# A Perceiver block on one core: contexts applied in one run, norm factors by ScalarE's root, and the copy of keys inside the maximum

## What is computed

```python
# cross attention: sublayers 1, 7 and 10 (a_cross, e_cross, t_cross), 16 heads of 8
att = softmax(einsum('bxhd,byhd->bhxy', q, k) * scale)    # 257 keys for each sequence
x = einsum('bhxy,byhd->bxhd', att, v) @ Wout + bout

# linear transformer: sublayer 2 (l), six layers deep, 8 heads of 16
q = softmax(q, axis=-1); k = softmax(k, axis=-2)
context = einsum('bhnd,bhne->bhde', k, v)
x = einsum('bhnd,bhde->bhne', q, context) @ wo[i] + bo[i] + x
hdn = layernorm(x) @ w1[i]; hdn = where(hdn >= 0, hdn, 0.01 * hdn)
x = hdn @ w2[i] + x

# mixtures of 8 experts: sublayers 3, 6 and 12 (a_moe, c_moe, u_moe)
normed = (xt - mu) * rsqrt(var + eps)      # u_moe: xt * rsqrt(mean(xt * xt) + eps), no mean
top_v, top_i = top_k(router(normed), 2)    # u_moe: one expert for each token
```

## Time and profile before

| | us |
|---|---|
| median of 3 runs | 4051.39 (4050.05 to 4054.77) |
| profiled execution | 4054.11 |
| its span, first to last instruction | 4052.3 |
| PE / PEld busy | 3461.1 / 2487.3 |
| DVE / ACT / POOL busy | 2627.4 / 2325.4 / 2470.0 |
| maximum of a_cross, first and last start | 19.4 to 504.5 |
| L3221 of the linear transformer, first and last start | 572.86 to 1351.57 (48) |
| maximum of e_cross, of t_cross | 2209.5 to 2693.4, 2953.7 to 3446.9 |
| PE busy, PE clock granted, 573 to 1352 | 761.00 of 779.00, 0.99 |
| the same, 20 to 500 | 458.35 of 480.00, 1.00 |
| PE busy and clock in a_moe's choice, 1373 to 1462 | 23.70 of 89.00, 0.51 |
| in c_moe's, 1908 to 1992 | 27.00 of 84.00, 0.52 |
| in u_moe's, 3877 to 3927 | 22.56 of 50.00, 0.53 |

### The profile page before, as it was taken

How to read it: one execution, slowest core, us unless ns; L and a number is a source line. 1 busy time by engine, 2 the same in 40 slices (tenths; PEclk the granted TensorE clock), 3 DMA queues, 4 the chain that set the end, 5 groups by cost and what they waited for, 6 DMA issues and landing times. The chain is left out here.

```text
span 4052.3 us, 120030 instructions
## 1 busy us (share of the span) xinstructions
PE 3461.1 (85%) x44674; PEld 2487.3 (61%) x44674; DVE 2627.4 (65%) x6958; ACT 2325.4 (57%) x6315; POOL 2470.0 (61%) x2844
## 2 busy tenths in 40 slices
PE   8999959999999669698498999978589999786866
PEld 6777737777777447455366777755367777453444
DVE  6777756666666423476434888767767777754655
ACT  6777736666566334287123777755567777544633
POOL 6676656666666543476424887756466766745633
PEclk9999979999999779899699999989599999887978
DMA  2111110000000122201122111110011110000023
GB/s 74 41 35 41 30 69 5 7 11 11 6 7 2 54 63 77 56 17 45 49 72 67 48 47 43 36 65 4 1 47 41 35 41 30 3 2 6 2 91 93
DMA packets 90550, 149.06 MB, mean 37 GB/s; under 512 B 10112, under 2 KB 66816, under 8 KB 89664
## 3 DMA queue, kind: packets, MB, share of 16 engines
q1 hardware_dynamic: 79936, 122.87, 9.8%
q0 software_dynamic: 10240, 20.99, 1.7%
HBM read 112.76 MB, written 31.06 MB: 35 GB/s over the span
## 5 line engine op out<-in xcount | busy, mean ns | idle before, releaser
L2228 POOL TENSOR_TENSOR t_cross_E<-t_cross_E,t_cross_inverse 128x1028 f32<-128x1028 f32 x128 | 243.2, 1900 | 139.7 <-DVE t_cross_inverse L2507 139.7
L2228 POOL TENSOR_TENSOR a_cross_E<-a_cross_E,a_cross_inverse 128x1028 f32<-128x1028 f32 x128 | 243.2, 1900 | 131.9 <-DVE a_cross_inverse L2507 131.9
L2454 ACT ACTIVATE t_cross_E<-t_cross_psum,t_cross_negtop 128x257 f32<-128x257 f32 x512 | 235.9, 474 | 134.6 <-DVE t_cross_negtop L2497 134.6
L2454 ACT ACTIVATE a_cross_E<-a_cross_psum,a_cross_negtop 128x257 f32<-128x257 f32 x512 | 236.0, 474 | 125.8 <-DVE a_cross_negtop L2497 125.8
L2454 ACT ACTIVATE e_cross_E<-e_cross_psum,e_cross_negtop 128x257 f32<-128x257 f32 x512 | 235.9, 474 | 124.2 <-DVE e_cross_negtop L2497 124.2
L2228 POOL TENSOR_TENSOR e_cross_E<-e_cross_E,e_cross_inverse 128x1028 f32<-128x1028 f32 x128 | 243.1, 1899 | 92.7 <-DVE e_cross_inverse L2507 92.7
L3065 PE MATMUL l_psum<-l_ffn_w,l_hidden 128*128 128x128 f32 x1536 | 219.5, 287 | 12.9 <-POOL l_hidden L2938 9.8
L3065 PEld LDWEIGHTS l_psum<-l_ffn_w,l_hidden 128*128 128x128 f32 x1536 | 192.1, 193 | 50.3 <-POOL l_hidden L2938 24.0
L3058 PE MATMUL l_psum<-l_hT,l_ffn_w 128*128 128x512 f32 x384 | 204.3, 635 | 0.9 <-ACT l_hT L3122 0.9
L2497 DVE TENSOR_REDUCE t_cross_negtop<-t_cross_psum 128x2 f32<-128x514 f32 x256 | 165.1, 687 | 47.7 <-PE t_cross_psum L2314 45.9
L2497 DVE TENSOR_REDUCE a_cross_negtop<-a_cross_psum 128x2 f32<-128x514 f32 x256 | 165.1, 686 | 40.3 <-PE a_cross_psum L2309 37.8
(11 more groups left out here) (754 smaller groups left out, 11137.2 us busy)
## 6 DMA issues: line engine op xcount, KB each, us to landing
a_cross_context<-context SPq DMA_DIRECT2D x32, 578.0 KB, 3.7
e_cross_context<-context SPq DMA_DIRECT2D x32, 578.0 KB, 3.7
t_cross_context<-context SPq DMA_DIRECT2D x32, 578.0 KB, 3.7
u_moe_weights<-pack_u_moe SPq DMA_DIRECT2D x1, 5633.0 KB, 16.7
slots<-l_blank SPq DMA_DIRECT2D x6, 832.0 KB, 12.0
a_moe_x_slots<-slots SPq DMA_DIRECT2D x26, 192.0 KB, 2.8
slots<-a_moe_y_slots SPq DMA_DIRECT2D x26, 192.0 KB, 2.0
c_moe_x_slots<-slots SPq DMA_DIRECT2D x26, 192.0 KB, 2.9
```

The costliest lines, as they stand in the source:

```text
L2228: pool.tensor_tensor(E[:, n % N], E[:, n % N], spread(inverse[:, n % 4], SK, 2), ALU.mult).then_inc(s_unit, 1)
L2454: act.activation(E[:, n % N, g], psum[:, g, 0:SK], ACT.Exp, bias=negtop[:, n % 2, g:g + 1], accum_out=total[:, n % 2, g:g + 1]).then_inc(s ...
```

## The change

Four edits. In the mixtures the factors leave POOL: ACT takes a root for two chunks at a time, DVE the reciprocal and the shift; DVE also applies the factors to chunks 1 and 3, and takes all statistics ahead of the first choice. In cross attention the copy of the keys moves between the two halves of the maximum. In the linear transformer the four quarters of attend stand in one run on PE, POOL does units after the leaky operations, and ACT copies aT ahead of raw 2.

```diff
@@ routed_experts
+    BY_VECTOR = (1, 3)
+    BY_SCALAR = tuple(c for c in range(CHUNKS) if c not in BY_VECTOR)
@@ gpsimd
-            def deviation(c):
...
-                last.then_inc(s_factor, 1)
             def put(g):
                 pool.wait_ge(s_place, g + 1)
                 for t in range(HALF):
-                    if g == 0 and t in (4, 8):
-                        deviation(PART + 1 + t // 4)
...
-            for c in range(PART + 2):
-                deviation(c)
@@ tensor
-                pe.wait_ge(s_norm, c + 1)
+                if c in BY_VECTOR:
+                    pe.wait_ge(s_normed, BY_VECTOR.index(c) + 1)
+                else:
+                    pe.wait_ge(s_norm, BY_SCALAR.index(c) + 1)
@@ scalar
+            def roots(u):
+                at = slice(2 * u * TPC, 2 * (u + 1) * TPC)
+                if rms:
+                    act.wait_ge(s_square, 4 * u + 4)
+                else:
+                    act.wait_ge(s_moments, 2 * u + 2)
+                first = square[:, at] if rms else moments[:, at, 1]
+                if twice:
+                    act.activation(root[:, at], first, ACT.Sqrt, scale=1.0 + 1e-5, bias=core.const("eps5_squared")).then_inc(s_root, 1)
+                else:
+                    act.activation(root[:, at], first, ACT.Sqrt, bias=core.const(eps)[:, 0:1]).then_inc(s_root, 1)
             def apply(c):
-                act.wait_ge(s_factor, c + 1)
+                act.wait_ge(s_factor, c // 2 + 1)
...
+            roots(0)
+            roots(1)
+            apply(0)
             router_arrived(act)
             for g in range(2):
-                apply(g * PART)
+                if g > 0:
+                    apply(g * PART)
                 for c in range(g * PART, (g + 1) * PART):
-                    if c + 1 < (g + 1) * PART:
+                    if c + 1 < (g + 1) * PART and c + 1 not in BY_VECTOR:
                         apply(c + 1)
                     turned(c)
+                    if c in (1, 2):
+                        roots(c + 1)
@@ vector
+            def factors(u):
+                at = slice(2 * u * TPC, 2 * (u + 1) * TPC)
+                dve.wait_ge(s_root, u + 1)
+                if rms:
+                    dve.reciprocal(factor[:, at], root[:, at]).then_inc(s_factor, 1)
+                else:
+                    dve.reciprocal(factor[:, at], root[:, at]).then_inc(s_inverse, 1)
+                    dve.wait_ge(s_inverse, u + 1)
+                    dve.scalar_tensor_tensor(out=shift[:, at], in0=moments[:, at, 0], scalar=-1.0, in1=factor[:, at],
+                                             op0=ALU.mult, op1=ALU.mult).then_inc(s_factor, 1)
+            def apply(c):
+                dve.wait_ge(s_factor, c // 2 + 1)
+                for at in range(c * TPC, (c + 1) * TPC):
+                    if rms:
+                        last = dve.tensor_scalar(rows[:, at], source[:, at], factor[:, at:at + 1], None, ALU.mult)
...
+                last.then_inc(s_normed, 1)
...
-            for c in range(PART + 2):
+            for c in range(PART):
                 statistics(c)
+            factors(0)
+            apply(1)
+            for c in range(PART, CHUNKS):
+                statistics(c)
+                if c == PART + 1:
+                    factors(1)
+                    apply(3)
             router_arrived(dve)
+            factors(2)
+            factors(3)
             choose(0)
             places(0)
-            for c in range(PART + 2, CHUNKS):
-                statistics(c)
             choose(1)
@@ cross_attention, vector
                 if exists(i, n):
-                    maximum(i, n)
+                    maximum(i, n, 0)
                 if exists(i, n + 1):
                     keys(i, n + 1)
+                if exists(i, n):
+                    maximum(i, n, 1)
@@ linear_transformer, gpsimd
-                if now.exists:
-                    units(now)
                 if two.exists:
                     leaky(two, 2)
                     leaky(two, 3)
+                if now.exists:
+                    units(now)
@@ linear_transformer, tensor
                 if one.exists:
-                    attend(one, 0)
+                    for t in range(TPC):
+                        attend(one, t)
                 if two.exists:
                     up(two, 2)
-                if one.exists:
-                    attend(one, 1)
-                if two.exists:
                     down(two, 0)
-                if one.exists:
-                    attend(one, 2)
-                if two.exists:
                     up(two, 3)
-                if one.exists:
-                    attend(one, 3)
-                if two.exists:
                     down(two, 1)
@@ linear_transformer, scalar
-                if two.exists:
-                    raw(two, 2)
                 if one.exists:
                     turned(C_BANK, aT[:], s_a, s_aT, one)
                 if two.exists:
+                    raw(two, 2)
                     raw(two, 3)
```

More of the change, by code:

```diff
@@ L72, in constants @@
     c["eps6"] = np.full((P, TPC), 1e-6)
+    c["eps5_squared"] = np.full((P, 1), 1e-10)
     c["own_place"] = (row[:, None] // S == np.arange(4)[None]).astype(float)
@@ L1377, in routed_experts @@
         square = sc.sb("square", [P, TILES]) if rms else None
-        var, rstd, factor, shift = [sc.sb(n, [P, TILES]) for n in ("var", "rstd", "factor", "shift")]
+        root, factor, shift = [sc.sb(n, [P, TILES]) for n in ("root", "factor", "shift")]
         fT = None if shared else sc.sb("fT", [P, 2, CHUNK])
-        s_stats, s_moments, s_square, s_dev = sc.sem("stats"), sc.sem("moments"), sc.sem("square"), sc.sem("dev")
+        s_stats, s_moments, s_square, s_root = sc.sem("stats"), sc.sem("moments"), sc.sem("square"), sc.sem("root")
+        s_inverse, s_normed = sc.sem("inverse"), sc.sem("normed")
         s_factor, s_norm, s_turned, s_fT, s_logits = (sc.sem("factor"), sc.sem("norm"), sc.sem("turned"), sc.sem("fT"),
@@ L1749, in statistics @@
                     dve.tensor_tensor(square[:, at], square[:, at], moments[:, at, 1], ALU.add).then_inc(s_square, 1)
+            def factors(u):
[13 more added lines that the diff above has]
+                        last = dve.tensor_scalar(rows[:, at], source[:, at], factor[:, at:at + 1], None, ALU.mult)
+                    else:
+                        last = dve.tensor_scalar(rows[:, at], source[:, at], factor[:, at:at + 1], shift[:, at:at + 1],
+                                                 ALU.mult, ALU.add)
+                last.then_inc(s_normed, 1)
             def choose(g):
@@ L2491, in _, with maximum @@
                 dve.tensor_scalar(mask_neg[:], mask_int[:], 0.0, -1e30, ALU.is_equal, ALU.mult).then_inc(s_mask_ready, 1)
-            def maximum(i, n):
-                dve.wait_ge(s_score, i * N + n + 1)
-                for half in range(2):
-                    at = slice(2 * half, 2 * half + 2)
-                    dve.tensor_reduce(negtop[:, n % 2, at], psum[:, at, 0:SK], AX.X, ALU.max, negate=True).then_inc(s_top, 1)
+            def maximum(i, n, half):
+                if half == 0:
+                    dve.wait_ge(s_score, i * N + n + 1)
+                at = slice(2 * half, 2 * half + 2)
+                dve.tensor_reduce(negtop[:, n % 2, at], psum[:, at, 0:SK], AX.X, ALU.max, negate=True).then_inc(s_top, 1)
             def first_half(i, n):
```

22 lines of the change are left out of this document (removed).

## The result

| | before | changed kernel |
|---|---|---|
| median, four runs each | 4053.08 us | 3989.06 us (3982.57 to 3990.99) |
| ratio, 95% interval | | 0.984, [0.9823, 0.9857] |
| profiled execution, span | 4054.11, 4052.3 | 3982.57, 3980.8 |

The time fell by 64 us, 1.6% and clear of noise, where 92 were forecast: inside the range, 27 us above the predicted 3962. The column "again" is a later profile of the same kernel. Stages that the change doesn't touch differ between two profiles of one kernel by up to 5 us (from the first matmul of c_self to that of c_moe 201.0 and 206.2).

A forecast was written before the change was run, and what follows sets the result against it. PE was taken to bound the linear transformer, a loop over DVE cross attention, POOL's puts a_moe and DVE's choice weights c_moe. From 4054.1 us, -40 (linear transformer), -28 (cross attention) and -24 (mixtures) gave 3962; range 3930 to 4005.

The forecast's parts named there:

- two of the prediction's own signs of being wrong: Forecast wrong if normal cross attention steps stay at 3.69 us or more, or PE's wait for leaky stays at 0.4.
- The two terms: Linear transformer, per step: attend in one run gains 0.60 us, units behind leaky 0.3; 0.9 x 45 steps gives -40.
- the four quarters one after another, 1.5 us: Linear transformer, PE: a sign to look for, the four attend quarters running consecutively in 1.5 us.
- The second term: Linear transformer: with units behind leaky, leaky 2 ends 1.0 us earlier, gaining 0.3 of PE's 0.46 wait per step.
- rival 2: Linear transformer: POOL becomes the bound, or small products in a run go slower; -12 instead of -40, 3990 us; chance 0.08.
- the copy starts when its projection has landed: Cross attention: the keys' copy starts about 0.6 us after the maximum began, so the transposes' wait for it ends 0.57 earlier.
- If the exponentials wait 0.15 longer than I think, three steps of four lose 0.08: Cross attention: the stated fragility of the -28 us, whose bounds were +10 and -58.
- The 0.10 in the sum for four steps: Cross attention: first of the gains 0.10 + 0.07 + 0 + 0.11 = 0.28 us per four steps, -27 over 96 groups.
- rival 1: Cross attention: the maximum's second half takes the place of the keys; +10 us there, 4000 in all; chance 0.13.
- Rival 4: Slower: in cross attention DVE waits for a late keys' projection, the maximum's half queued behind; 4117 us at 0.4 late; chance 0.04.
- the +64: Cross attention: what the forecast -28 us becomes if the keys' projection lands 0.3 us later than read.
- the part would have been -11: Mixtures: estimate by the skill page, instead of -24 us, if the five added table switches lay in the open.

The follow-up runs named there:

- dve_leaky: The changed kernel with one of POOL's two leaky operations, that of hidden tile 2, moved to the end of DVE's step: 3978.12 us, ratio 0.9822.
- et_odd: The changed kernel with ScalarE copying the second transposes ahead of the values in odd steps of cross attention only: 3981.06 us, ratio 0.9823.
- et_first: The changed kernel with ScalarE copying the second transposes ahead of the values in all steps of cross attention: 4040.78 us, ratio 0.9946.
- mix_only: The kernel before with the mixtures' part of the change alone (root and reciprocal): 4044.65 us, ratio 0.9953.
- keys_only: The kernel before with the cross attention's part alone, the keys' copy between the maximum's halves: 4055.13 us, ratio 0.9986.
- linear_only: The kernel before with the three edits of the linear transformer alone: 4029.59 us, ratio 0.9927.

## Why the prediction was right, and where it was off

The time lies inside the range, but two of the prediction's own signs of being wrong came: normal steps of cross attention took 3.62 to 3.80 us, most of them over 3.69, and PE's wait for leaky grew from 0.46 to 0.64. The mechanism held in the mixtures and in half of the linear transformer, and failed in cross attention.

*Linear transformer, -40 against -34.4 (about -31 without the step at the lowered clock).* The two terms were gains of 0.60 and 0.3 a step; they measured 0.90 and -0.12 (the mean distance from the first turn to down went from 0.81 to 0.93, pure 0.44). That their sum came near is luck: one was too small by 0.3, the other too large by 0.4. Of the first, the four products came out as forecast, 3.61 against 3.60; mis-sized was the run itself, for which "the four quarters one after another, 1.5 us" stood and 1.21 came. The Trainium skill, "TensorEngine Tiling (Array Packing)", Key Properties, says that a change of tiling mode drains the engine. The trace agrees: with three fewer entries and exits each product is about 0.15 shorter, and the quarters themselves 0.3 together, though it can't tell a drain from another cost of the change. The second term failed at "then asks for it about when it is there": PE came earlier still, and POOL sets the pace. That is rival 2's mechanism, at a small price: 15 us, by dve_leaky, where rival 2 had 28.

*Cross attention, -28 against -8.* This is the step that failed: "the copy starts when its projection has landed: that starts 0.66 behind the scores in a normal step". The 0.66 was a row of before, and I took it for PE's own pace. With the exponentials 0.15 later ACT's copy of the second transposes is later behind the scores, and with it the projection, the copy of the keys, the maximum's second half and the next exponentials: a ring, of which I had walked half. et_odd and et_first show the link from that copy to the projection: with the bank free early, the projection of a normal step starts 0.65 behind the scores in a_cross and e_cross, and in et_odd such a step takes 3.61, where 3.62 was forecast. That later exponentials delay the copy is read from ACT's timeline; no run moved them alone. "If the exponentials wait 0.15 longer than I think, three steps of four lose 0.08" was nearly the right price (they lost 0.05 each); it should have been the main case. The 0.10 in the sum for four steps had no working. The range held it, between the forecast and rival 1 (4000). Rival 4's lateness came to 0.16, and its price was wrong: by its own formula 0.16 costs 384 x (0.16 - 0.07) = 35 us, where the stages gained 8; and the +64 that it names for 0.3 is reached at 0.24.

*Mixtures, -24 against -22.8.* a_moe -14.7 and c_moe -11.0 against -13.6 and -10.8: the first put 7.1 earlier and 1.0 later (forecast 5.5 and 1.2), the puts at an even pace, the table load in idle time. By the Trainium skill ("ScalarE: Activation LUTs", What ACT_TABLE_LOAD costs: 2.66 us for each switch) the part would have been -11, an estimate, if the switches lay open. The trace has the load at 1.28 and none of it in the sum. Nor does it show the drain where ScalarE has work ready: before, in a stage that the change doesn't touch, the next activation starts 1.32 us behind the end of the one ahead (2730.15 to 2731.47):

```profile
2729.67 0.48 ACT L1116 ACTIVATE retention_normed<-X,retention_shift,retention_rstd 128x128 f32<-128x128 f32 x1
2730.18 1.28 ACT L1129 ACT_TABLE_LOAD   x1
2731.47 0.60 ACT L1129 ACTIVATE retention_gate<-retention_psum 128x512 f32<-128x512 f32 x1
```

So an open switch costs about 1.3 us here, half of the page's figure, and the five would have cost 7 us, not 13. u_moe was +2.9 against +1. The first put was 3.6 late (forecast 4), and the puts without deviations 2.6 shorter (forecast 2.4); not foreseen were the 3.2 of the long addition in their middle. The rest, 1.3 less from the last put to the experts, closes the sum.

Still open: why the clock falls after some of PE's pauses and not after others.

## What to carry to other kernels

A distance read between two instructions is a price only if nothing in the changed order can hold the second: before shifting an operation, follow the bank or buffer that it needs through every engine, and around the loop back to the operation itself. When two edits meet at one wait, price them together: here about 5 and 9 us alone were 31 together. Look at the granted clock and at single long steps before you compare two stages: here they were worth up to 7 us. And work that comes earlier meets other work, as DVE's long addition did POOL's puts.

## What was not expected of the hardware

A put that runs into DVE's addition of two 128x4096 tensors in SBUF took 4.13 us, in another kernel 5.06, instead of 0.96; before, when that addition (4.42 us) ran behind the puts, the longest put of the stage took 1.13. In both kernels the put ends 0.84 us behind the addition (3849.38 after 3848.54, 3828.27 after 3827.43), however early it began, as if held until then; in the changed kernel the put ahead of it (3843.99), under way when the addition started (3844.12), took its usual 0.96. The Trainium skill, "GPSIMD Engine Reference", 1. Specifications, lists GpSimd's SBUF interfaces as shared with VectorE, with contention where an instruction has two SBUF inputs; the trace agrees.

In mix_only's profile DVE's chain of small dependent operations at the end of c_moe's choice had gaps of 0.3 to 1.3 us ahead of most of its operations, while puts ran beside it and for 5 us after the last one (it ended at 1967.75), and took 31 us (1945.00 to 1975.95):

```profile
1950.64 0.18 DVE L1846 COPY c_moe_tot_b<-c_moe_tot 128x32 f32<-128x32 f32 x1 [0.99 <-DVE c_moe_tot L1729]
...
1952.75 0.20 DVE L1846 COPY c_moe_tot<-c_moe_tot_b 128x64 f32<-128x64 f32 x1 [1.01 <-DVE c_moe_tot_b L1729]
```

In the changed kernel the same chain, with puts beside it too, has no gaps and takes 12.8 us:

```profile
1906.13 0.18 DVE L1846 COPY c_moe_tot_b<-c_moe_tot 128x32 f32<-128x32 f32 x1
...
1906.77 0.20 DVE L1846 COPY c_moe_tot<-c_moe_tot_b 128x64 f32<-128x64 f32 x1
```

In mix_only the experts waited for this chain, which explains c_moe's smaller gain in that run. The gaps aren't the edit's: between the first MEMSET of c_moe_tot and the second c_moe_rank they sum to 19.2 us in mix_only and 19.1 in et_first, 1.6 in keys_only and 1.7 in linear_only, whose chain starts when nearly all puts are done, and 0 in the ten other profiles. These four are the first group, beside which the kernel before took 11 to 13 us longer than beside the others. So something of that group's time was at work; what it was isn't known. It makes that group's totals less sure than their intervals say, and is a reason to go by stages there.
